# Queries of a cross-attention: Wq's splits in front of the third tile of rows, own banks for the second turned tile, turns of the identity in pauses

## The reference

```python
# x: (32, 32, 1024), ctx: (32, 257, 1024), all float32
x = x + xattn(layernorm(x), ctx, ctx, Wq, Wk, Wv, Wo)     # 32 heads, 8 key/value heads, head size 32
x = x + attn(layernorm(x), eta)                           # y y^T over the 32 rows of each batch
x = x + ffn(layernorm(x), gate_w, expert_w)               # 8 experts, 2 chosen per row, 1024 x 1024 each

def xattn(query, key, value, Wq, Wk, Wv, Wo):
    q = (query @ Wq)  # (32, 32, 1024) @ (1024, 1024), split into heads
    k, v = key @ Wk, value @ Wv       # (32, 257, 1024) @ (1024, 256)
    probs = softmax(q k^T * 32**-0.5)
    return (probs v) @ Wo
```

## Time and profile before

| | |
|---|---|
| timed runs | 1123.93, 1124.9 and 1117.28 us, median 1123.93 |
| the profiled execution's own time | 1120.3 us |
| its span, first to last instruction | 1118.8 us |
| mean granted clock of TensorE | 0.979 |
| busy: TensorE, its weight loads, VectorE, ScalarE, GpSimd | 94%, 86%, 59%, 40%, 24% |

### The profile page before, as it was taken

How to read it: one execution, slowest core, us unless ns; L and a number is a source line. 1 busy time by engine, 2 the same in 40 slices (tenths; PEclk the granted TensorE clock), 3 DMA queues, 4 the chain that set the end, 5 groups by cost and what they waited for, 6 DMA issues and landing times. The chain is left out here.

```text
span 1118.8 us, 25717 instructions
## 1 busy us (share of the span) xinstructions
PE 1054.3 (94%) x8958; PEld 963.3 (86%) x8959; DVE 663.0 (59%) x1672; ACT 449.4 (40%) x1087; POOL 269.4 (24%) x452
## 2 busy tenths in 40 slices
PE   5799989999999999999999999599997898999997
PEld 5799989999999999999999998487775687877886
DVE  6452236667666666666666666657786554465351
ACT  3231225555555555554555555423324033333120
POOL 2000102111111111112111120044454243333343
PEclk9999989999999999999999999699998899999999
DMA  9144366756556575666656646355547655577532
GB/s 333 46 162 152 109 189 182 207 153 207 170 173 200 163 207 164 182 180 181 204 155 193 175 142 194 124 210 91 106 126 245 239 207 219 181 284 279 173 96 73
DMA packets 82748, 197.88 MB, mean 177 GB/s; under 512 B 18608, under 2 KB 29232, under 8 KB 78544
## 3 DMA queue, kind: packets, MB, share of 16 engines
q1 hardware_dynamic: 64672, 154.15, 44.3%
q0 software_dynamic: 17968, 42.29, 12.2%
HBM read 159.69 MB, written 44.56 MB: 183 GB/s over the span
## 5 line engine op out<-in xcount | busy, mean ns | idle before, releaser
L451 ACT ACTIVATE prob<-bank,nmax 128x257 f32<-128x257 f32 x256 | 122.0, 477 | 243.3 <-DVE nmax L591 243.1
L591 DVE TENSOR_REDUCE nmax<-bank 128x1 f32<-128x257 f32 x256 | 108.7, 425 | 159.7 <-PE bank L784 159.7
L671 PE MATMUL bank<-cT_h,wkv_h 128*128 128x256 f32 x512 | 155.2, 303 | 0.0
L680 PE MATMUL bank<-wkv_h,cT_h 128*128 128x256 f32 x512 | 154.4, 302 | 0.0
L671 PE MATMUL bank<-cT_h,wkv_l 128*128 128x256 f32 x512 | 145.3, 284 | 0.0
L671 PE MATMUL bank<-cT_l,wkv_h 128*128 128x256 f32 x512 | 144.9, 283 | 0.0
L680 PE MATMUL bank<-wkv_h,cT_l 128*128 128x256 f32 x512 | 144.5, 282 | 0.0
L680 PE MATMUL bank<-wkv_l,cT_h 128*128 128x256 f32 x512 | 143.9, 281 | 0.0
L344 POOL DMA_DIRECT2D qcat<-q_scratch x128 | 70.2, 555 | 273.1 <-PE bank L784 270.1
L706 PE MATMUL bank<-ident,prob 128*128 128x128 f32 x512 | 101.1, 279 | 10.1 <-DVE pT L244 6.8
L1669 PE MATMUL bank<-w_h,rows_h 128*128 x272 | 107.9, 397 | 0.0
(11 more groups left out here) (212 smaller groups left out, 2423.8 us busy)
## 6 DMA issues: line engine op xcount, KB each, us to landing
kcat<-k_scratch SPq DMA_DIRECT2D x128, 258.0 KB, 4.2
cx<-in_context SPq DMA_DIRECT2D x32, 1024.0 KB, 7.4
raw<-in_expert_w SPq DMA_DIRECT2D x48, 512.0 KB, 6.7
qcat<-q_scratch POOLq DMA_DIRECT2D x128, 128.0 KB, 3.2
k_scratch<-kT_h SPq DMA_DIRECT2D x32, 258.0 KB, 2.7
k_scratch<-kT_l SPq DMA_DIRECT2D x32, 258.0 KB, 2.9
x_in<-in_x SPq DMA_DIRECT2D x16, 512.0 KB, 7.0
expert_raw<-in_expert_w SPq DMA_DIRECT2D x16, 512.0 KB, 10.1
```

The costliest lines, as they stand in the source:

```text
L451: act.activation(prob[:, 1 - par, s, 0:SK], s_ps[s % 2][:, 0:SK], ACT.Exp, bias=nmax[:, 1 - par, s:s + 1], accum_out=sums[:, 1 - par, s:s ...
L591: dve.reduce_max(nmax[:, 1 - par, s:s + 1], s_ps[s % 2][:, 0:SK], AXX, negate=True).then_inc(max_done, 1)
L671: o = pe.matmul(k_ps[:, j * 256:(j + 1) * 256], wkv[w][:, k, j * P:(j + 1) * P], cT[t][:, b % 2, k, :], start=(j == 0 and k == 0 and n == ...
L680: o = pe.matmul(v_ps[:, a * KV:(a + 1) * KV], cT[t][:, b % 2, k, a * P:(a + 1) * P], wkv[w][:, k, KV:2 * KV], start=(a == 0 and k == 0 and ...
```

## The change

Six edits, all in `attend`:

- SyncE loads x's second tile in front of Wq's first chunk, not behind it.
- GpSimd's three memsets wait until two tiles are normalized.
- ScalarE splits all of Wq in front of the third tile's high part; wq_high(0) now stands in front of x_high(0), and wq_high(1) between x_high(0) and x_high(1).
- VectorE normalizes tile 0 in front of the statistics of tile 1, does wq_low(0) in front of normalizing tile 1, and all other splits of Wq in front of x_low(2).
- Tile 1 is turned into banks 6 and 7, all others into 0 and 1; `turn_x(1)` waits for no low part.
- TensorE turns the identity itself, into bank 5, whose content nobody reads: 38 times ahead of tile 0, 16 times behind it, 8 times behind tile 1.

```diff
-        xT_ps = banks[0:2]
+        xT_ps = lambda t: banks[6:8] if t == 1 else banks[0:2]
+        warm_ps = banks[5]
...
             load_x(0)
+            load_x(1)
             for c in range(KC):
                 sp.dma_start(wq_raw[:, c, :], wq[c * P:(c + 1) * P, :]).then_inc(chunk_loaded[c], 16)
-                if c == 0:
-                    load_x(1)
             load_x(2)
             load_x(3)
...
             for t in range(2):
                 norm.on_gpsimd(pool, t)
+            pool.wait_ge(xn_ready, 2)
             pool.memset(zeros[:, :], 0.0).then_inc(zeros_ready, 1)
...
+            wq_high(0)
             x_high(0)
-            wq_high(0)
+            wq_high(1)
             x_high(1)
-            wq_high(1, 2, 3, 4)
+            wq_high(2, 3, 4, 5, 6, 7)
             x_high(2)
-            wq_high(5, 6)
             x_high(3)
-            wq_high(7)
             q_high(0, 0, 1, 2, 3)
...
             statistics(0)
+            normalized(0)
             statistics(1)
-            normalized(0)
+            wq_low(0)
             normalized(1)
             x_low(0)
-            wq_low(0)
             x_low(1)
-            wq_low(1, 2)
+            wq_low(1, 2, 3)
             statistics(2)
-            wq_low(3)
+            wq_low(4)
             normalized(2)
-            wq_low(4)
+            wq_low(5)
             statistics(3)
-            wq_low(5)
+            wq_low(6)
             normalized(3)
+            wq_low(7)
             x_low(2)
-            wq_low(6)
             x_low(3)
-            wq_low(7)
...
             def turn_x(t):
                 pe.wait_ge(xn_ready, t + 1)
                 for k in range(KC):
-                    if k % 4 == 0 and t >= 1:
+                    if k % 4 == 0 and t >= 2:
                         pe.wait_ge(xT_l_ready, 2 * t - 1 + k // 4)
-                    o = pe.transpose(xT_ps[k // 4][:, k % 4 * P:(k % 4 + 1) * P], xn[:, t % 2, k * P:(k + 1) * P], ident[:, :])
+                    o = pe.transpose(xT_ps(t)[k // 4][:, k % 4 * P:(k % 4 + 1) * P], xn[:, t % 2, k * P:(k + 1) * P], ident[:, :])
...
+            def keep_busy(turns):
+                for _ in range(turns):
+                    pe.transpose(warm_ps[:, 0:P], ident[:, :], ident[:, :])
+
             pe.wait_ge(ident_ready, 1)
+            keep_busy(38)
             turn_x(0)
+            keep_busy(16)
             turn_x(1)
+            keep_busy(8)
             first_queries(0, 1, 2, 3, 4)
```

More of the change, by code:

```diff
@@ L378, in x_high @@
                     act.activation(xT[g % 2][0][:, 4 * h:4 * h + 4, t % 2 * P:(t % 2 + 1) * P],
-                                   xT_ps[h][:, :].rearrange("p (k n) -> p k n", n=P), ACT.Copy).then_inc(xT_h_ready, 1)
+                                   xT_ps(t)[h][:, :].rearrange("p (k n) -> p k n", n=P), ACT.Copy).then_inc(xT_h_ready, 1)
             def wq_high(*chunks):
@@ L429, in _ @@
             act.wait_ge(clT_done, 1)
-            act.activation(clT[0][:, :, 0:B], xT_ps[0][:, 0:KC * B].rearrange("p (k b) -> p k b", b=B), ACT.Copy).then_inc(clT_h_ready, 1)
+            act.activation(clT[0][:, :, 0:B], xT_ps(0)[0][:, 0:KC * B].rearrange("p (k b) -> p k b", b=B), ACT.Copy).then_inc(clT_h_ready, 1)
             q_high(3, 2, 3)
@@ L494, in x_low @@
                     rows = (slice(None), slice(4 * h, 4 * h + 4), slice(t % 2 * P, (t % 2 + 1) * P))
-                    dve.tensor_tensor(xT[g % 2][1][rows], xT_ps[h][:, :].rearrange("p (k n) -> p k n", n=P),
+                    dve.tensor_tensor(xT[g % 2][1][rows], xT_ps(t)[h][:, :].rearrange("p (k n) -> p k n", n=P),
                                       xT[g % 2][0][rows].bitcast(F32), ALU.subtract).then_inc(xT_l_ready, 1)
@@ L567, in _ @@
             dve.wait_ge(clT_h_ready, 1)
-            dve.tensor_tensor(clT[1][:, :, 0:B], xT_ps[0][:, 0:KC * B].rearrange("p (k b) -> p k b", b=B),
+            dve.tensor_tensor(clT[1][:, :, 0:B], xT_ps(0)[0][:, 0:KC * B].rearrange("p (k b) -> p k b", b=B),
                               clT[0][:, :, 0:B].bitcast(F32), ALU.subtract).then_inc(clT_l_ready, 1)
@@ L751, in _ @@
             for k in range(KC):
-                o = pe.transpose(xT_ps[0][:, k * B:(k + 1) * B], cl[:, k * P:(k + 1) * P], ident[0:B, 0:B])
+                o = pe.transpose(xT_ps(0)[0][:, k * B:(k + 1) * B], cl[:, k * P:(k + 1) * P], ident[0:B, 0:B])
             o.then_inc(clT_done, 1)
```

## The result

| | before | after |
|---|---|---|
| median of 15 timed runs each | 1127.08 us (1117.28 to 1132.31) | 1114.15 us (1109.26 to 1118.49) |
| ratio, 95% interval | | 0.990 [0.988, 0.9919] |
| the profiled execution | 1120.3, span 1118.8 | 1114.3, span 1112.8 |

A forecast was written before the change was run, and what follows sets the result against it. The prediction took the start of the second group's queries on TensorE (49.81 us) as the bound: 6.4 us from pauses less 2.8 for a later first product gives 3.6, so 1121.6 - 3.6 = 1118.0 us, range 1109 to 1123.

The forecast's parts named there:

- the two pauses: TensorE's two waits on wq_l behind tile 2's turns and ahead of 46.83: both go, 2 x 3.1 = 6.2 us gained.
- the last split at 30.7: On VectorE, the last split of Wq ends at 30.7 us, 3.5 to 6 us before TensorE wants chunks 4 to 7.
- the earlier normalized tiles: On VectorE, tile 0 is normalized from 7.3 instead of 9.55 us, and tile 1 ready at 12.3 instead of 12.67.
- no rise from turns: On TensorE, identity turns don't raise the clock; the first product comes 2.8 us later, at 18.8; chance 0.58.
- the product of 49.81: TensorE's start of the second group's queries, at 49.81 us before; forecast at 46.2; what it gains, the end gains.
- Rival A: The turns at TensorE's start raise the clock: first product at 14.5, gain 10.2 us, time 1111.4; chance 0.30.
- the 5.46 us: Time from the kernel before's first product to its clock rise, read as no earlier than 5.3 us without turns at 152.83.
- The row at 883.60: Trace place in the last stage where eight turns, then products brought the clock's rise in 5.0 us; taken as undecided.
- Rival C: Clock falls in the last stage's waits for gathered rows make it slower, up to 1127; chance 0.07 together with another rival.
- 1118.0: The forecast time of the whole changed kernel in us, 1121.6 - 3.6, with its own range 1113.5 to 1122.5.
- The gain of 3.6 us: Forecast gain of the whole change: 6.4 us from the pauses less 2.8 us for a later first product.
- the 1121.6: Starting time for the forecast: mean in us of the kernel before's three timed runs and its profiled execution.

The follow-up runs named there:

- e3: The kernel before with only the splits of Wq moved ahead of the third tile's high and low parts: 1114.75 us, ratio 0.9907.
- e7: The changed kernel with the 38 turns of the identity but without the 16 and the 8: 1114.98 us, ratio 0.9924 to the kernel before.
- e9: The changed kernel with turns of the identity also in five later pauses, 44 of them ahead of the first scores: 1111.25 us, ratio 0.9893.
- e12: The same kernel as e3 (only the splits of Wq moved), timed once more beside the changed kernel: 1118.79 us, ratio 0.994 to the kernel before.
- e5: The kernel before once more, unchanged, for a second trace: profiled execution 1132.75 us.
- e11: The changed kernel once more, unchanged, timed beside other kernels on one chip: 1115.85 us, ratio 0.9933 to the kernel before.
- e2: The kernel before with only the 38, 16 and 8 turns of the identity added: 1124.22 us, ratio 0.9998.
- e4: The changed kernel with the splits of Wq's chunks 5 to 7 put back: 1124.89 us, ratio 1.0012 to the kernel before.
- e6: The changed kernel once more, unchanged, for a second trace: profiled execution 1114.4 us.
- e8: The changed kernel with turns of the identity also in five later pauses, 24 ahead of the first scores: 1109.03 us, ratio 0.9859.

## Why the prediction was right, and where it was wrong

*Right: the two pauses.* 6.2 us, 6.4 with the slower products behind them, and no new wait; e3 and the waits after show it, and e3's mark gives 6.8 for them (7.1 earlier, of which 0.35 by an earlier first product). The sum that put the last split at 30.7 was a step short: tile 2's 0.8 us isn't in the 25.1. The split ends at 29.3 all the same, as the splits ahead of tile 2 came sooner than I added up (tile 2 is normalized at 22.07, not by 23.9).

*Right: the earlier normalized tiles,* with small errors: tile 0 at 7.01 where I wrote 7.3, tile 1 ready at 11.9 where I wrote 12.3.

*Wrong: "no rise from turns",* the step on which the likeliest case stood. The clock rises an estimated 3.2 us after the first turn in one trace and 5.4 in another (e7), and in e9 it stays at 1.00 through 4.6 us of turns alone. The forecast's own consequences were then all wrong: 38 turns were to end at 10.1 and ended at 7.6, the first product was to come at 18.8 and came at 14.11, the product of 49.81 at 46.2 and came at 38.96. Rival A had 14.5 and 39.6 for them and a gain of 10.2 us; measured at the mark, 10.85. The reason I gave for it was the start of the kernel before, where 16 turns in front of the first product seemed to bring nothing. e7 points at what I had overlooked: turns and pauses alternate there, 1.0 and 0.7 us in the earlier trace rows, and pauses can undo what turns do; with 38 turns in front and then pauses of 2.3 and 1.1 us the first product was slow too. That the shorter pauses of the kernel before did the same there is argued and not shown. I also took the 5.46 us for more exact than it is: with no turns of the identity in front, the clock rises 4.6 (e12) to 6.1 us (e5) after the first product. The Trainium skill (TensorE: Matmul & The Clock Gate, Part 4: PE-mode transpose), by which turning doesn't engage the upper clock, is at odds with these traces, and the traces decide. The row at 883.60, which I had called undecided, was the better witness.

*Rival C,* falls of the clock in the last stage, was half of the mechanism, and for the wrong thing: together with the length of the waits for gathered rows, the larger part between before and e5, it goes with the scatter of the runs (271.4 against 263.6 us with one and the same kernel), and isn't seen as a cost of the change.

*Luck: how near 1118.0 lies.* The gain of 3.6 us was too small by 9.3 against the 12.9 of the medians, and the 1121.6 it was taken from was 5.5 below the median of before, 1127.08. The two errors cancel in part, and 1114.15 is 3.9 us off.

*The sum at the end.* 10.85 us at the mark and 12.9 by the medians of the first comparison, but 9.7 by those of e11's (1125.54 and 1115.85): the mark lies between them, and what is left is no more than the scatter. That nothing behind the mark changes is shown by TensorE's equal busy time up to the first gathered tile, and behind it no more closely than the scatter allows.

*Not foreseen:* that a pause of 2.9 us costs more than its length where the clock falls behind it. In both traces of before it didn't fall there, in e2 and e4 it did, twice each. What decides between the two stays open; the pauses have the same length, but stand at other times. The length of a single wait doesn't decide it either: behind 1.40 us at 872.44 in the changed kernel the clock was low, behind 2.73 at 887.15 in e6 it was not.

## What to carry to other kernels

Read the pitch of equal instructions (the time from the start of one to the start of the next), not only the clock's row: the row said 1.00 for a stretch that ran at half of it, and the pitch showed it. Work without use ahead of TensorE's first real work is worth the slow stretch behind (2.4 us here, seen at the mark), but only if the pauses between it and that work are filled or removed too; remove first the pauses that come from an order of lists, here 6.2 of 10.85 us. And before reading a difference of a few microseconds at the end, take the same kernel's trace twice: here one stage alone differed by 7 to 8 us between executions of one kernel.

## What the hardware showed beyond that

Turns of 128 x 128 blocks against the identity have a pitch of 0.107 and 0.217 us at the two clocks. The clock rises under them after an estimated 3.1 to 5.4 us in the nine executions that begin with 38 of them; counted from the first product, in the five that don't, after 4.6 to 6.1 us. It falls behind pauses of 2.9 us in e2 and e4 and not in before, and behind one of 2.3 us in e8. The normalization of a tile took 1.59 us beside GpSimd's memsets and 0.81 without them. And the turn of a tile of gathered rows waits 0 to 5.5 us for the same transfer in different executions, 5.5 us of scatter at a single place, and more where the clock then falls.
